# Shared key tiles, idle products, and a new order in local attention's opening turn, in a one-core decoder layer

## What is computed

```
x = x + retention(layernorm(x))              # 16 heads of 8: causal scores, divided by exp(n), no softmax
x = x + cross(layernorm(x), context)         # 16 heads of 8: o = sigmoid(q k^T / sqrt(8)) v over 1601 keys
x = x + ffn(layernorm(x)):                   # two layers of:
      x = x + local(shift_token(x)) wo       # 8 heads of 64, window 64, l2-normed and rotated q and k, softmax
      x = x + gelu-gate(layernorm(shift_token(x)))
```

## Time and profile before

| | us |
|---|---|
| median of three timed runs | 1788.67 (1788.62 to 1791.8) |
| the profiled execution | 1783.75 |
| its span in the trace | 1781.9 |
| n1, retention | 0 to 27, 27 to 150 |
| n2, cross-attention's opening | 150.4 to 177.4, 177.6 to 190.2 |
| cross-attention's sigmoid loop | 190.2 to 1028 |
| n3 | 1031.5 to 1051.6 |
| local layer 0, local layer 1 | 1051.8 to 1416.7, 1417 to 1781.9 |
| busy: TensorE, VectorE, ScalarE, GpSimd | 1685.1, 1019.3, 1424.7, 454.7 |

### The profile page before, as it was taken

How to read it: one execution, slowest core, us unless ns; L and a number is a source line. 1 busy time by engine, 2 the same in 40 slices (tenths; PEclk the granted TensorE clock), 3 DMA queues, 4 the chain that set the end, 5 groups by cost and what they waited for, 6 DMA issues and landing times. The chain is left out here.

```text
span 1781.9 us, 66416 instructions
## 1 busy us (share of the span) xinstructions
PE 1685.1 (95%) x28128; PEld 1019.0 (57%) x28128; DVE 1019.3 (57%) x3178; ACT 1424.7 (80%) x2649; POOL 454.7 (26%) x387
## 2 busy tenths in 40 slices
PE   7998899999999999999999978999999979999998
PEld 4785555555555555555555435666663346666643
DVE  4566543333443333344333058999984489999954
ACT  4444899999999999999999957888884368898852
POOL 1115000000000000000000027777730177877500
PEclk9999999999999999999999989999999999999999
DMA  2000311111111111111110030111110001111100
GB/s 63 1 0 25 125 50 50 64 51 45 64 65 50 50 51 49 61 64 55 54 36 32 3 113 20 34 36 24 32 34 15 0 19 32 27 35 32 31 18 36
DMA packets 47421, 73.33 MB, mean 41 GB/s; under 512 B 8400, under 2 KB 38224, under 8 KB 47184
## 3 DMA queue, kind: packets, MB, share of 16 engines
q1 hardware_dynamic: 47184, 69.85, 12.7%
HBM read 21.08 MB, written 2.10 MB: 13 GB/s over the span
## 5 line engine op out<-in xcount | busy, mean ns | idle before, releaser
L690 ACT ACTIVATE x_probs<-x_pss 128x1024 f32<-128x1024 f32 x832 | 806.4, 1021 | 35.3 <-PE x_pss L611 4.0
L625 PE MATMUL x_acc<-x_probs,x_v 128*32 128x256 f32 x6656 | 435.8, 379 | 0.0
L611 PE MATMUL x_pss<-x_qx,x_kx 32*128 32x256 bf16 x9984 | 347.0, 269 | 6.9 <-ACT x_probs L690 2.1
L611 PEld LDWEIGHTS x_pss<-x_qx,x_kx 32*128 32x128 bf16 x9984 | 221.8, 93 | 189.9 <-ACT x_probs L690 171.2
L625 PEld LDWEIGHTS x_acc<-x_probs,x_v 128*32 128x32 f32 x6656 | 207.9, 110 | 82.9 <-issue 5.3
L737 DVE COPY x_vnext<-x_psp 128x128 f32<-128x128 f32 (+1 forms) x197 | 58.2, 295 | 314.3 <-PE x_psp L589 313.8
L1520 ACT ACTIVATE l_prob<-l_neg_sim,l_neg_top 128x128 f32<-128x128 f32 x512 | 198.6, 396 | 6.0 <-DVE l_neg_top L1334 6.0
L951 POOL TENSOR_TENSOR l_turned_half<-l_raw,l_tabB 128x512 f32<-128x512 f32 x128 | 186.3, 1477 | 49.2 <-ACT l_raw L1479 46.7
L666 POOL COPY x_zq<-zT 128x256 f32<-128x256 f32 x15 | 6.0, 403 | 746.3 <-PE x_psp L596 680.6
L961 POOL TENSOR_TENSOR l_direct<-l_direct,l_turned_half 128x1024 f32<-128x1024 f32 x64 | 151.5, 2367 | 0.0
L1334 DVE CUSTOM_DVE_ANT_0 l_neg_sim<-l_pss,w_window,l_inv_norm 128x128 f32<-128x128 f32 x512 | 149.1, 348 | 3.5 <-issue 2.8
(11 more groups left out here) (206 smaller groups left out, 2622.0 us busy)
## 6 DMA issues: line engine op xcount, KB each, us to landing
x_kx<-x_kp SPq DMA_DIRECT2D x96, 208.0 KB, 2.3
x_cT<-in_context SPq DMA_DIRECT2D x16, 832.0 KB, 4.6
x_qx<-x_qp SPq DMA_DIRECT2D x48, 192.0 KB, 2.3
l_vmid<-l_vt SPq DMA_DIRECT2D x64, 128.0 KB, 2.3
xT<-in_x SPq DMA_DIRECT2D x8, 256.0 KB, 6.3
shifted<-zT SPq DMA_DIRECT2D x32, 64.0 KB, 2.0
hs<-zT SPq DMA_DIRECT2D x32, 64.0 KB, 2.0
out_x<-xT SPq DMA_DIRECT2D x8, 256.0 KB, 2.0
```

What stands on the lines that cost most here:

```text
L611: ins = pe.matmul(pss[bank(k, 2 * p + r // 2)][:, r % 2, e, :], kx[par][rows, g, j * P:(j + 1) * P], qx[par][rows, g, a * S:(a + 1) * S], ...
L625: ins = pe.matmul(acc[32 * r:32 * r + 32, 0:S], v[:, j, g, r, :], probs[SLOT[p]][r // 2][:, r % 2, e, :], start=(u == 0), stop=(u == UNITS ...
L690: act.activation(probs[SLOT[p]][y][:, :, :, :], pss[bank(k, 2 * p + y)][:, :, :, :], ACT.Sigmoid, scale=HD ** -0.5).then_inc(weighed, 1)
```

## The change

Three things are changed together.

Key tiles: per group 12 full tiles remain (MT), 24 pairs. The 65 keys left over per group are taken out. 64 of them (TAIL) share two units: pair TAILS has two groups per unit, each on 64 of the 128 columns, so its score is 48 products of 32x64. The last key of all groups and heads goes to pair LONE: GpSimd builds a small tile `klone` whose 32 columns per group hold each head's last key and nothing else; the score is 12 products, the sigmoid one ACTIVATE of 256 columns, the mix 4 products with `vlone`, which VectorE builds. A batch still has 26 turns and the same 24 + 2 pieces; the last value piece projects two tiles. VectorE has three more instructions per batch (`set_tails`).

Idle products: `keep_warm` becomes `idle_products`, and its calls are put into more places: 5 before `variances(1)`, WARM 8 to 11, 4 after `widen(1)` in each norm; 4 before retention's first projection, 11 after its first turn, 5 after its loop; 6, 5 and 3 in cross-attention's opening; 6 before a local layer's turns, 4 + 3 + 3 in turn -1, 4 + 8 in turn 0.

Opening: in turn -1 of a local layer GpSimd does turn_halves(0,1), join(0,0), join(0,1), scale_keys(0,1), turn_halves(1,0). VectorE scales the keys of (0,0) itself (`scale_first_keys`) and has `floor_of` first in its queue; ScalarE's roots and TensorE's project_k(1,1) come earlier.

```diff
-VCH = [(0, 4), (4, 7), (7, 10), (10, 13)]
+VCH = [(0, 4), (4, 8), (8, 12), (12, 14)]
+def idle_products(pe, ones_mean, to, times):
+    for _ in range(times):
+        pe.matmul(to, ones_mean[:, :], ones_mean[:, :], start=True, stop=True)
...
+            idle_products(pe, ones_mean, var[1][:, 0:P], 5)
             variances(1)
             widen(0)
-            keep_warm(WARM)
+            idle_products(pe, ones_mean, mean[0][:, 0:P], WARM)
             widen(1)
+            idle_products(pe, ones_mean, mean[0][:, 0:P], 4)
...
+            def first_turn_or_turn(n, u):
+                turn(n, u)
+                if isinstance(n, int) and n == 0:
+                    idle(11)
+            idle(4)
             project(0, 0)
             project(1, 1)
-            turns(pe, turn)
+            turns(pe, first_turn_or_turn)
+            idle(5)
...
+    MAIN = HG * MT // 2
+    PAIRS = MAIN + 2
+    TAILS, LONE = MAIN, MAIN + 1
+    WEIGHTS = 2 * PAIRS - 1
...
-                for r in range(HL):
-                    ins = pe.matmul(psp[32 * r:32 * r + 32, 0:D], cT[par][:, j * P + 32 * r:j * P + 32 * r + 32],
-                                    w["wv"][:, :], start=True, stop=True)
+                for i in ((j,) if j < MT else (MT, MT + 1)):
+                    for lo, at in tokens_of(i, 32):
+                        ins = pe.matmul(psp[lo:lo + 32, (i - j) * D:(i - j + 1) * D], cT[par][:, at:at + 32],
+                                        w["wv"][:, :], start=True, stop=True)
...
+                if p == LONE:
+                    score_lone(n, par)
+                    return
...
+                    if p < TAILS:
+                        g, j = divmod(2 * p + e, MT)
+                        parts = [(0, P, g, j * P)]
+                    else:
+                        parts = [(lo, TAIL, 2 * e + lo // TAIL, MT * P) for lo in (0, TAIL)]
                     for a in range(PARTS):
+                        for lo, size, g, key in parts:
+                            for r in range(HL):
+                                rows = slice(32 * r, 32 * r + 32)
+                                ins = pe.matmul(pss[bank(2 * p + r // 2)][lo:lo + size, r % 2, e, :],
+                                                kx[par][rows, g, key:key + size],
+                                                qx[par][rows, g, a * S:(a + 1) * S], start=(a == 0), stop=(a == PARTS - 1))
+            def score_lone(n, par):
+                pe.wait_ge(lone_ready, n + 1)
+                pe.wait_ge(weighed, n * WEIGHTS + 2 * LONE - 2)
+                for a in range(PARTS):
+                    for g in range(HG):
+                        ins = pe.matmul(pss[bank(2 * LONE)][32 * g:32 * g + 32, 0, 0, :], klone[par][:, g, :],
+                                        qx[par][:, g, a * S:(a + 1) * S], start=(a == 0), stop=(a == PARTS - 1))
+                ins.then_inc(scored, 1)
...
             project_first()
-            score(0, 0, 0, 0, 0)
+            idle(5)
+            score(0, 0, 0, 0)
+            idle(3)
...
+                    if p == LONE:
+                        act.activation(probs[SLOT[p]][0][:, 0, 0, :], pss[bank(2 * p)][:, 0, 0, :], ACT.Sigmoid,
+                                       scale=HD ** -0.5).then_inc(weighed, 1)
...
+            def opening(x):                       # GpSimd, turn -1 of a local layer
+                turn_halves(later(x, 1), 1)
+                join(later(x, 1), 0)
+                join(later(x, 1), 1)
+                scale_keys(later(x, 1), 1)
+                turn_halves(later(x, 2), 0)
...
+            def scale_first_keys(x, t):           # VectorE
+                n, r, _ = x
+                dve.wait_ge(newton, 4 * n + 4)
+                dve.wait_ge(joined, 2 * n + t + 1)
+                dve.tensor_tensor(direct[r % 2][t][:, FH:QK, :], direct[r % 2][t][:, FH:QK, :],
+                                  inv_norm[r % 2][:, t, FH:QK].unsqueeze(2).broadcast_to([P, FH, FD]),
+                                  ALU.mult).then_inc(scaled[t], 1)
+            def opening(x):                       # VectorE, turn -1
+                floor_of(later(x, 1))
+                multiply_q(later(x, 2), 0)
+                multiply_k(later(x, 2), 0)
+                inverse_norms(later(x, 1))
+                multiply_q(later(x, 2), 1)
+                scale_first_keys(later(x, 1), 0)
+                sums(later(x, 2), 0)
+                multiply_k(later(x, 2), 1)
+                place_keys(later(x, 1), 0)
+                place_keys(later(x, 1), 1)
+                sums(later(x, 2), 1)
+                copy_v(later(x, 1), 0)
+                mask(later(x, 1), 0, 0)
...
+                idle(x, -1, 4)                    # TensorE, in the local turn
                 project_q(later(x, 2), 1)
...
+                idle(x, 0, 4)
                 score(x, 1)
                 value(later(x, -1), 1)
+                opening = isinstance(x[0], int) and x[0] == -1
+                if opening:
+                    project_k(later(x, 2), 1)
+                idle(x, -1, 3)
                 flip_q(later(x, 1), 0)
                 turn_over(x, 0, 0)
-                project_k(later(x, 2), 1)
+                if not opening:
+                    project_k(later(x, 2), 1)
                 project_out(later(x, -1))
+                idle(x, -1, 3)
+                idle(x, 0, 8)
                 flip_k(later(x, 1), 0)
```

More of the change, by code:

```diff
@@ L59, in layer_norm @@
     norms["runs"] += 1
-    base, NG, WARM = run * NCH, NCH // 4, 8
+    base, NG, WARM = run * NCH, NCH // 4, 11
     mean_ready, centered, square_ready, var_ready, log_ready, guess_ready, newton, spread, normed = norms["sems"]
@@ L501, in out_use, with bank, tokens_of @@
             return uses_before(n + 1) + OUT_AT + c
-        def bank(k, h):
-            return (k + h) % 3
+        def bank(h):
+            return h % 3
+        def tokens_of(j, rows):
+            if j < MT:
+                return [(lo, j * P + lo) for lo in range(0, P, rows)]
+            if j == MT:
+                return [(lo, j * P + lo % TAIL) for lo in range(0, P, rows)]
+            return [(lo, LASTKEY) for lo in range(0, P, rows)]
         def turns(eng, body):
             for n in range(B):
-                body(n, n % 2, n // 2, n % 3, last=n == B - 1)
+                body(n, n % 2, n // 2, last=n == B - 1)
         @block.sync
@@ L617, in mix @@
                     pe.wait_ge(o_ready, n)
[L618 to L623, removed]
-                    for r in range(HL):
-                        ins = pe.matmul(acc[32 * r:32 * r + 32, 0:S], v[:, j, g, r, :],
-                                        probs[SLOT[p]][r // 2][:, r % 2, e, :], start=(u == 0), stop=(u == UNITS - 1))
+                pe.wait_ge(weighed, n * WEIGHTS + (2 * p + 2 if p < LONE else WEIGHTS))
@@ new lines, in mix @@
+                if p >= TAILS:
+                    pe.wait_ge(v_set, n * SETS + HG + 2 + (p - TAILS))
+                for e in range(2 if p < LONE else 1):
+                    g, j = divmod(2 * p + e, MT)
+                    if p < TAILS and j == 0:
+                        pe.wait_ge(v_set, n * SETS + g + 1)
+                    for r in range(HL):
+                        if p < TAILS:
+                            values = v[:, j, g, r, :]
+                        elif p == TAILS:
+                            values = vtail[:, (e * HL + r) * 32:(e * HL + r + 1) * 32]
+                        else:
+                            values = vlone[:, r, :, :].rearrange("p g d -> p (g d)")
+                        ins = pe.matmul(acc[32 * r:32 * r + 32, 0:S], values,
+                                        probs[SLOT[p]][r // 2 if p < LONE else 0][:, r % 2 if p < LONE else 0, e, :],
+                                        start=(p == 0 and e == 0), stop=(p == LONE))
@@ L627, in mix, with turn @@
                 ins.then_inc(mixed, 1)
-            def turn(n, par, half, k, last=False):
+            def turn(n, par, half, last=False):
                 first = isinstance(n, int) and n == 0
@@ L788, in _ @@
                 set_values(0, g, V0)
+            set_tails(0, V0)
             turns(dve, turn)
@@ L1227, in chunk, with idle @@
                 widen(n, 2)
+            def idle(x, n, times):
+                if isinstance(x[0], int) and x[0] == n:
+                    idle_products(pe, ones_mean, pso[:, 0, :], times)
             assert HC == 3
+            idle_products(pe, ones_mean, pso[:, 0, :], 6)
             turns(pe, turn, 4)
@@ L1537, in turn @@
                 exps(x, 0, 0)
+                opening = isinstance(x[0], int) and x[0] == -1
+                if opening:
+                    roots(later(x, 1))
                 squares(later(x, 2), 0)
@@ L1540, in turn @@
                 copy(later(x, -1), 1, 0)
-                roots(later(x, 1))
+                if not opening:
+                    roots(later(x, 1))
                 copy_out(later(x, -1), 0)
@@ L1655, in build @@
```

(4 more changed lines are left out.)

118 lines of the change are left out of this document (80 added, 38 removed).

## The result

The changed kernel takes 1771.47 us in the median of four runs (1767.93 to 1774.7) against 1788.64 before (1788.01 to 1791.8): ratio 0.9904, 95% interval 0.9885 to 0.9923. In a second set of runs, beside 11 of before, the ratio was 0.9912 (0.9887 to 0.9937). It is 16 to 17 us faster; 6.5 were forecast, with a range of 1768 to 1793 for the time. The profiled executions differ by less: 1783.75 before, 1771.81 after (span 1770.0), 11.9 us.

A forecast was written before the change was run, and what follows sets the result against it. TensorE was taken to bound cross-attention's loop, ScalarE just under it. Cross-attention -2.9, clock -6.3, idle products' cost +0.3, retention's branch +2.4, opening order 0: -6.5 us, from 1788.67 to 1782.2, range 1768 to 1793.

The forecast's parts named there:

- The bound of cross-attention: Cross-attention's sigmoid loop: TensorE sets the pace, ScalarE's loop lies 0.01 to 0.1 us under it per turn.
- Rival 1: Cross-attention: ScalarE alone is the bound, about 1.7 us saved per batch, 27 in all, giving 1758 us; chance 0.07.
- rival 2: Cross-attention: TAILS' products run four abreast, 0.76 us more per batch, +5.5 in all, giving 1794 us; chance 0.09.
- Its size: Cross-attention's gain: 0.1 us per batch, 1.5 in all, plus 1.4 behind the last batch; -2.9 us (bounds -0.5 and -4.1).
- the turn with LONE's score: End of a cross-attention batch: score 0.41, piece 0.24, mix 0.98, together 1.63 us; with TAILS' turn 3.86 against 3.96.
- The branch: Retention's loop entry: TensorE branches only after the eleven idle products are issued, delaying the first score; +2.4 us (0 to 2.6).
- rival 4: Retention's loop entry: the branch runs beside the eleven idle products, so nothing is lost; -8.9 us in all, 1779.8; chance 0.13.
- The clock: Idle products remove eight of ten half-clock stretches, each priced between 0 and 1.7 us; -6.3 us (bounds 0 and -13.6).
- Rival 3: Idle products don't hold the clock, or its falls move elsewhere; 1788.5 us, no change; chance 0.16.
- The order of the opening: Local layers' opening turns: the new order alone gives nothing; 0 us (bounds -0.7 and +1.5 per layer).
- The baseline: Start of the sum: timed median 1788.67 us, 4.9 above the profiled execution, from which the forecast 6.5 was subtracted.
- the clock's full price: Half-clock stretches: 1.7 us each where TensorE alone holds the path; in half of them, this set the range's lower end.

## Why the prediction was right in its direction and too small

**The bound of cross-attention: right.** ScalarE gave up 1.7 us per batch and the batch became 0.4 shorter. Rival 1 is out, and so is rival 2: 48 products of 32x64 in 0.79. In both kernels each of the four row groups writes 512 fp32 columns of its own in the `pss` tiles (`pss[bank(2 * p + r // 2)][.., r % 2, ..]`), so nothing here shows what row groups that share a part of PSUM would do.

**Its size: wrong.** The step that failed is "the turn with LONE's score 0.41 + 0.24 + 0.98 = 1.63", which took 1.53, together with "1.98 + 0.25 = 2.23" for TAILS' turn, which took 2.11, and with the 3.96 before, which was 4.04. I had added parts that were measured between other neighbours. The 0.98 of a mix and the 0.76 of a score each contain a change of tile shape, and LONE's score spares two of them. Per batch 0.40 at the boundary and 0.02 in the next turn, in place of 0.1; behind the last batch 1.2 of the forecast 1.4. The loop's -7.7 lies outside the bounds that I gave, -0.5 and -4.1.

**The branch: wrong.** "The branch's row is nearer to the first: +2.4." The row said that the branch begins when the turn's last products are issued; I read into it that it cannot begin earlier. With products of 0.24 us in the queue it began 2 us before their end. For this term rival 4 was the right one.

**The clock: right where TensorE alone holds the path** (n2 1.7, cross-attention's opening 1.1, retention's start 1.6, all of it ahead of the first turn's scores, 33.75 before and 32.14 now). Rival 3 is out: the idle products alone gave 5 to 6 us. In the local layers turn 0 won 1.0 and 1.15, from 16.89 and 17.08 to 15.9, more than the 0.45 that I gave; but layer 0's opening kept both of its low stretches (21.15 us from projection to score instead of 21.65, and 19.88 at full clock), and the six products cost 1.9 in layer 0 and 1.4 in layer 1, where I had put nothing. Layer 1's opening kept one as well, at a place where it cost nothing: 19.88 instead of 21.09. Nothing of the forecast named SyncE's queue in n3, which I had not opened.

**The order of the opening: right.** 19.89 and 19.88. The steps are there as worked out: floor_of (L1436) is held until the first join has ended, inverse_norms (L1444) until the second; scale_first_keys (L1456) takes 1.15 beside scale_keys, and 0.68 in layer 0, where it began 0.1 before scale_keys ended. GpSimd and VectorE in layer 1's opening after the change:

```profile
1415.57 4.67 POOL L1064 TENSOR_TENSOR l_direct<-l_direct,l_turned_half 128x1024 f32<-128x1024 f32 x2
1420.83 1.04 POOL L1073 TENSOR_TENSOR l_direct<-l_direct,l_inv_norm 128x512 f32<-128x512 f32 x1 [0.58 <-DVE l_inv_norm L1449]
...
1416.44 1.54 DVE L1436 SCALAR_TENSOR_TENSOR l_sumsq<-l_sumsq 128x32 f32<-128x32 f32 x1
1419.10 1.19 DVE L1444 SCALAR_TENSOR_TENSOR l_tmp_a<-l_root,l_sumsq 128x32 f32<-128x32 f32 x1
1421.27 1.15 DVE L1456 TENSOR_TENSOR l_direct<-l_direct,l_inv_norm 128x512 f32<-128x512 f32 x1
```

**The baseline.** I subtracted from the median what I had read in one execution. That execution had a mean clock of 0.990, the median one 0.987; after the change the four on record have 0.995 to 1.000. I had seen the 4.9 us between the two and carried them along as a constant.

**Luck.** The time lies in the recorded range, 1768 to 1793, but not in the forecast's own, 1778 to 1787. The lower end was set for the clock's full price in half of the stretches; what filled it was mostly cross-attention, the branch and the baseline, three terms that were wrong in the same direction.

## What to carry to other kernels

Price a group of products between the neighbours that it will have: if its tile shape is that of the products around it, it is cheaper than half of a group that isn't. Where the clock is at stake, one profiled execution is a sample: compare its mean clock with those of the timed executions before a gain from it is put on the median. Filler products pay where TensorE alone resumes the path; before building a filler for a stage, open the queue that ends the stage, here SyncE's.

## What the runs showed of the hardware

A change of tile shape between consecutive products on TensorE cost 0.10 to 0.12 us (0.86 and 0.98 for the same mix, 0.33 and 0.43 for the same twelve products). TensorE's sequencer entered a loop's branch 2 us before the products ahead of it had ended. The low clock can last: 10.2 us in a row in the run without the eleven products, where those of the profiled pair, the end of the kernel left out, had 3.4 each. And the executions of the kernel before span 11 us, 1783.0 to 1794.2, with mean clocks of 0.989 to 0.984.
